# x split tile by tile on GpSimd, and t1 kept centred with its mean beside it, in a two-phase attention and FFN kernel

## The reference

```python
x = einsum('oc,bchw->bohw', inv(I - tpl), x)      # channel mixing by an inverted circulant, "conv"
t = to_tokens(x)                                   # 16 x 1024 tokens x 128
q, k = elu(ln(t) Wq) + 1, elu(ln(t) Wk) + 1;  v = ln(t) Wv         # 8 heads of 16
t = t + causal_linear_attention(q, k, v) @ W_out.T
z = ln(t)
g = mean_over_tokens(relu(z @ gfc1.T + b) @ gfc2.T + b)            # 8 gates for each batch
W1m, W2m = W1 + g . tv_W1, W2 + g . tv_W2                          # weights of their own per batch
t = t + ln(z + relu(z @ W1m.T + b1m) @ W2m.T + b2m) * lng + lnb
```

## Time and profile before

| what | value |
|---|---|
| median of 3 runs | 747.53 us (747.09 to 748.32) |
| the profiled execution | 749.55 us, of which the span of the profile is 747.8 us |
| mean granted TensorE clock | 0.975 |
| busy, of the span | PE 93%, DVE 88%, ACT 87%, POOL 62% |
| first phase at an even pace | 110 to 470 us |
| second phase, first 8 batches | about 500 to 592 us |

### The profile page before, as it was taken

How to read it: one execution, slowest core, us unless ns; L and a number is a source line. 1 busy time by engine, 2 the same in 40 slices (tenths; PEclk the granted TensorE clock), 3 DMA queues, 4 the chain that set the end, 5 groups by cost and what they waited for, 6 DMA issues and landing times. The chain is left out here.

```text
span 747.8 us, 38168 instructions
## 1 busy us (share of the span) xinstructions
PE 692.5 (93%) x12002; PEld 533.8 (71%) x12002; DVE 659.1 (88%) x2409; ACT 649.1 (87%) x1780; POOL 465.2 (62%) x790
## 2 busy tenths in 40 slices
PE   4898899999999999999999999888999998999993
PEld 2576677777777777777777777775777787777772
DVE  5697889999999999999999999768898977998983
ACT  4797989999999999999999999557888876888883
POOL 3686778888888888888888888421333321333333
PEclk9798999999999999999999999899999999999998
DMA  4757676666666666666666666410222211222221
GB/s 149 112 110 134 132 129 129 148 143 131 148 142 132 148 141 132 148 141 134 148 139 135 148 142 123 74 51 1 73 85 83 71 58 31 85 70 84 84 84 70
DMA packets 202485, 82.66 MB, mean 111 GB/s; under 512 B 176093, under 2 KB 189824, under 8 KB 202377
## 3 DMA queue, kind: packets, MB, share of 16 engines
q1 hardware_dynamic: 202440, 82.08, 48.3%
HBM read 22.79 MB, written 17.30 MB: 54 GB/s over the span
## 5 line engine op out<-in xcount | busy, mean ns | idle before, releaser
L892 DVE SCALAR_TENSOR_TENSOR scores_lo<-p_a,scores_hi 128x512 f16<-128x512 f32 x256 | 173.3, 683 | 1.7 <-ACT scores_hi L786 1.3
L786 ACT ACTIVATE scores_hi<-p_a 128x512 f16<-128x512 f32 x256 | 156.2, 611 | 9.3 <-PE p_a L623 9.3
L1010 POOL CAST qk_parts<-qk_f 128x512 f16<-128x512 f32 x128 | 78.0, 610 | 50.2 <-issue 24.9
L1442 POOL TENSOR_TENSOR ffn_rstd_shift<-ffn_rstd_shift,consts 128x4 f32<-128x4 f32 x32 | 36.5, 1142 | 109.1 <-DVE ffn_rstd_shift L1400 109.1
L984 POOL TENSOR_TENSOR stats<-stats,consts 128x2 f32<-128x2 f32 (+1 forms) x128 | 88.2, 689 | 17.9 <-DVE stats L925 13.1
L1224 PE MATMUL psb<-merged_W_of_batch,h_hi 128*128 128x128 f16 x512 | 94.5, 220 | 2.2 <-DVE h_lo L1378 1.5
L1378 DVE TENSOR_TENSOR h_lo<-h_f,h_hi 128x512 f16<-128x512 f32 x128 | 95.6, 786 | 1.1 <-ACT h_hi L1280 1.1
L1269 ACT ACTIVATE h_f<-psb,merged_b_of_batch 128x512 f32<-128x512 f32 x128 | 87.2, 709 | 10.3 <-PE psb L1205 8.6
L1225 PE MATMUL psb<-merged_W_of_batch,h_hi 128*128 128x128 f16 x512 | 94.2, 220 | 0.0
L1226 PE MATMUL psb<-merged_W_of_batch,h_lo 128*128 128x128 f16 x512 | 94.1, 220 | 0.0
L1016 POOL TENSOR_TENSOR qk_parts<-qk_f,qk_parts 128x256 f16<-128x256 f32 x128 | 85.9, 671 | 10.2
(11 more groups left out here) (215 smaller groups left out, 2697.5 us busy)
## 6 DMA issues: line engine op xcount, KB each, us to landing
x_f<-in_x SPq DMA_DIRECT2D x32, 256.0 KB, 3.2
t_rows<-t SPq DMA_DIRECT2D x64, 128.0 KB, 1.8
t_back<-t_rows SPq DMA_DIRECT2D x32, 256.0 KB, 2.6
out<-out_tile SPq DMA_DIRECT2D x32, 256.0 KB, 2.1
tv_share<-in_L_ffn_tv_W SPq DMA_DIRECT2D x32, 128.0 KB, 2.2
qkT_parts<-qk_parts SPq DMA_TRANSPOSE x128, 3.1
zT_hi_lo<-z_parts SPq DMA_TRANSPOSE x128, 2.3
merged_W<-in_L_ffn_W SPq DMA_DIRECT2D x2, 256.0 KB, 4.4
```

The costliest lines, as they stand in the source:

```text
L786: nc.scalar.activation(ah[:, t % 2, cols], p_a[:, cols], ACT.Relu).then_inc(ahi_ready[eo], 1)
L892: nc.vector.scalar_tensor_tensor(al[:, t % 2, cols], p_a[:, cols], 0.0, ah[:, t % 2, cols], ALU.max, ALU.subtract).then_inc(alo_ready[eo], 1)
```

## The change

Four edits.

1. `split_x` leaves ScalarE. GpSimd now makes both parts, one tile at a time and with skew -1, that is for the tile of the next slot: `x_hi` (a cast, 128 x 128) and `x_lo` (a subtraction, 128 x 128) in each slot. GpSimd's loop ends one batch earlier for that, and the last batch is written out.
2. The inverse is centred over its output channels (`centred_inverse` was there already for the projections), W_out has the mean of each row taken off, and one more column holds those means. `out_project` so gives t1 less its mean in columns 0 to 127 and its mean in column 128. `conv` uses the same centred columns.
3. ScalarE's z is then one product of t1 with rstd, with no bias; the stage `shift2` on DVE goes, with its semaphore.
4. In the second phase `add_up` is four operations of 128 x 128, each t1 + mean + normed. The rows of t1 in DRAM are 129 wide.

The lists of ScalarE and VectorE are also put in another order.

```diff
-SCALAR_ORDER = [("normalise", 10), ("split_x", 0), ("relu_qk", 2), ("read_t1", 7), ("gate_relu", 14),
-                ("exp_qk", 1), ("state_hi", 3), ("v_hi", 1), ("tv_hi", 0), ("scores_hi_0", 4), ("copy_out", 6),
-                ("scores_hi_1", 4)]
+SCALAR_ORDER = [("relu_qk", 2), ("normalise", 10), ("read_t1", 7), ("gate_relu", 14), ("v_hi", 1), ("tv_hi", 0),
+                ("state_hi", 3), ("exp_qk", 1), ("scores_hi_0", 4), ("copy_out", 6), ("scores_hi_1", 4)]
...
-        woT = sb(top, "w_outT", [P, C])
+        woT = sb(top, "w_outT", [P, C + 1])
...
-            yt = sb(early, "t1", [P, TILES, C])
+            yt = sb(early, "t1_centred_and_mean", [P, TILES, C + 1])
...
+                    nc.vector.scalar_tensor_tensor(wbig[:, 4 * C:4 * C + 1], pa[:, 1, 0:1], WSI, wbig[:, 3 * C:3 * C + 1],
+                                                   ALU.mult, ALU.subtract)
                     dve.wait_ge(s_wtc, 1)
-                    nc.vector.tensor_scalar(woT[:, :], wsqT[:, 3, :], WSI, None, ALU.mult)
+                    link(nc.vector.tensor_reduce(v[:, 15:16], wsqT[:, 3, :], AX.X, ALU.add))
...
+                    link(nc.vector.tensor_scalar(woT[:, C:C + 1], v[:, 15:16], WSI / C, None, ALU.mult))
+                    nc.vector.tensor_scalar(woT[:, 0:C], wsqT[:, 3, :], WSI, woT[:, C:C + 1], ALU.mult, ALU.subtract)
...
-                        o, cols = p_m1[:, 0:P], slice(j * P, (j + 1) * P)
-                        mm(o, xh[:, hf, cols], wh[:, 0:C], start=True, stop=False)
+                        o, cols = p_m1[:, 0:C + 1], slice(j * P, (j + 1) * P)
+                        mm(o, xh[:, hf, cols], wh[:, 3 * C:4 * C + 1], start=True, stop=False)
...
-                        nc.scalar.activation(xh[:, hf, cols], xf[:, hf, cols], ACT.Copy).then_inc(xh_ready, 1)
...
-                        act.wait_ge(shift_ready, n + 1)
+                        act.wait_ge(rstd, n + 1 + PAIRED)
                         at_least(act, zlo_ready, n - 1)
-                        nc.scalar.activation(z_[:, t % 2, :], yt[:, t, :], ACT.Identity, bias=st2[:, (t + 3) % 4, SHIFT:SHIFT + 1],
-                                             scale=st2[:, (t + 3) % 4, RSTD:RSTD + 1]).then_inc(z_ready, 1)
+                        nc.scalar.activation(z_[:, t % 2, :], yt[:, t, 0:C], ACT.Copy, scale=st2[:, (t + 3) % 4, RSTD:RSTD + 1])\
+                            .then_inc(z_ready, 1)
...
-                    def split_x(b, t):
-                        if t % 2 or isinstance(b, int) and TILES * b + t == 0:
+                    def x_hi(b, t):
...
+                        if j == 0:
+                            pool.wait_ge(x_loaded[hf], loaded)
+                        at_least(pool, wo_done, used)
+                        nc.gpsimd.tensor_copy(xh[:, hf, cols], xf[:, hf, cols]).then_inc(xh_ready, 1)
+                    def x_lo(b, t):
...
+                        pool.wait_ge(xh_ready, n + 1)
                         nc.gpsimd.tensor_tensor(xl[:, hf, cols], xf[:, hf, cols], xh[:, hf, cols], ALU.subtract)\
                             .then_inc(xl_ready, 1)
...
-                        nc.vector.tensor_tensor(rn[:, hf, :, :], rn[:, hf, :, :], t1b[:, hf, :, :], ALU.add)\
-                            .then_inc(v_ready, 1)
+                        for j in range(HALF):
+                            last = nc.vector.scalar_tensor_tensor(rn[:, hf, j, :], t1b[:, hf, j, 0:C], t1b[:, hf, j, C:C + 1],
+                                                                  rn[:, hf, j, :], ALU.add, ALU.add)
+                        last.then_inc(v_ready, 1)
```

More of the change, by code:

```diff
@@ L43 @@
                 ("gate", 13), ("project", 0)]
-SCALAR_ORDER = [("normalise", 10), ("split_x", 0), ("relu_qk", 2), ("read_t1", 7), ("gate_relu", 14),
-                ("exp_qk", 1), ("state_hi", 3), ("v_hi", 1), ("tv_hi", 0), ("scores_hi_0", 4), ("copy_out", 6),
-                ("scores_hi_1", 4)]
[L47 to L50, removed]
+SCALAR_ORDER = [("relu_qk", 2), ("normalise", 10), ("read_t1", 7), ("gate_relu", 14), ("v_hi", 1), ("tv_hi", 0),
+                ("state_hi", 3), ("exp_qk", 1), ("scores_hi_0", 4), ("copy_out", 6), ("scores_hi_1", 4)]
+VECTOR_ORDER = [("make_qk", 2), ("tv_lo", 1), ("divide", 6), ("stats2", 7), ("v_lo", 2), ("stats1", 0),
+                ("mean_var2", 7), ("mean_var1", 0), ("state_lo", 3), ("scores_lo_0", 4), ("denominator", 5),
+                ("scores_lo_1", 4), ("invert", 5)]
+GPSIMD_ORDER = [("rsqrt", 1), ("z_hi", 10), ("x_hi", -1), ("z_lo", 10), ("qk_hi", 2), ("x_lo", -1), ("qk_lo", 2),
                 ("last_rsqrt2", 8)]
@@ L146, in build @@
         delta2h = sb(top, "delta2_f16", [P, GB, FI], F16)
-        wh = sb(top, "w_in_hi", [P, 4 * C], F16)
-        wl = sb(top, "w_in_lo", [P, 4 * C], F16)
-        woT = sb(top, "w_outT", [P, C])
+        wh = sb(top, "w_in_hi", [P, 4 * C + 1], F16)
+        wl = sb(top, "w_in_lo", [P, 4 * C + 1], F16)
+        woT = sb(top, "w_outT", [P, C + 1])
         gfh = sb(top, "gate1_hi", [P, C], F16)
@@ L349, in _ @@
                     act.wait_ge(x_loaded[0], 16)
-                    nc.scalar.activation(xh[:, 0, 0:2 * P], xf[:, 0, 0:2 * P], ACT.Copy).then_inc(xh_ready, 1)
+                    nc.scalar.activation(xh[:, 0, 0:2 * P], xf[:, 0, 0:2 * P], ACT.Copy).then_inc(xh_ready, 2)
                     act.wait_ge(ln_done, 1)
@@ L438, in batch, with run @@
                         behind(TILES * (b - B) + slot)
-            def run(eng, order, stages, behind=None):
+            def run(eng, order, stages, behind=None, upto=B):
                 stages = [(skew, stages[name]) for name, skew in order]
@@ L443, in run @@
                     batch(stages, b)
-                with eng.Fori(2, B) as b:
+                with eng.Fori(2, upto) as b:
                     batch(stages, b)
-                for b in range(B, B + 2):
-                    batch(stages, b, behind)
-            MEAN, VAR, RSTD, SHIFT = 9, 10, 11, 12
+                for b in range(upto, B + 2):
+                    batch(stages, b, behind if b >= B else None)
+            MEAN, VAR, RSTD = 9, 10, 11
             PAIRED = 7
@@ L748, in read_t1 @@
                         act.wait_ge(wo_done, n + 1)
-                        nc.scalar.activation(yt[:, t, :], p_m1[:, 0:P], ACT.Copy, scale=1.0 / WSI).then_inc(t1_ready, 1)
+                        nc.scalar.activation(yt[:, t, :], p_m1[:, 0:C + 1], ACT.Copy, scale=1.0 / WSI).then_inc(t1_ready, 1)
                     def v_hi(b, t):
@@ L823, in merged_w1_hi @@
                             .then_inc(mhi_ready, 1)
-                    run(act, SCALAR_ORDER, {"tv_hi": tv_hi, "split_x": split_x, "read_t1": read_t1, "v_hi": v_hi,
+                    run(act, SCALAR_ORDER, {"tv_hi": tv_hi, "read_t1": read_t1, "v_hi": v_hi,
                         "exp_qk": exp_qk, "relu_qk": relu_qk,
@@ L966, in _ @@
                     run(dve, VECTOR_ORDER, {"tv_lo": tv_lo, "stats1": stats1, "mean_var1": mean_var1, "v_lo": v_lo,
[L967 removed]
+                        "make_qk": make_qk, "state_lo": state_lo,
                         "scores_lo_0": scores_lo(0), "scores_lo_1": scores_lo(1), "denominator": denominator,
@@ L1045, in _ @@
                     run(pool, GPSIMD_ORDER, {"rsqrt": rsqrt, "qk_lo": qk_lo,
-                        "split_x": split_x,
-                        "last_rsqrt2": last_rsqrt2, "qk_hi": qk_hi, "z_hi": z_hi, "z_lo": z_lo})
+                        "x_hi": x_hi, "x_lo": x_lo,
+                        "last_rsqrt2": last_rsqrt2, "qk_hi": qk_hi, "z_hi": z_hi, "z_lo": z_lo}, upto=B - 1)
         with ExitStack() as pb:
```

81 lines of the change are left out of this document (37 added, 44 removed).

## The result

The changed kernel takes **757.29 us** (median, 755.58 to 758.23), the kernel before 747.92 us on the same chip. The ratio is **1.0129** (95% interval 1.0109 to 1.0148). The forecast was 732 us with a range of 719 to 754, so it had the wrong sign and missed by 25 us. The profiled execution took 758.23 us with a span of 756.4 us, which is 8.6 us more than the span before. Medians here are of the fast executions; one of the ten of e4 was slow (880.8 us, granted clock 0.665) and is left out.

What follows compares the result with a forecast made beforehand. It took ScalarE, with DVE and PE 2 to 3% behind, to bound the first phase, and a ring of DVE and GpSimd the second. -21 + 5.6 + 0.5 = -15 us from 747.53 gave 732 us, range 719 to 754.

Steps and rivals of the forecast that it cites:

- PE's need: First phase: PE could do a slot in 3.20 us (3.16 to 3.25), the rest of its 3.48 being waiting.
- 3.20 by starts, 3.33 by durations: First phase: two sums for GpSimd's work per slot after the change; 3.25 us was taken, ends 3.20 and 3.45.
- the half that I counted as won: First phase, DVE: tv_lo's hold-up by GpSimd, 0.10 us on a mean slot, of which half, 0.05 us, was counted as won.
- four engines between 3.19 and 3.25 us to a slot of 3.30: First phase: the engines' needs overlap imperfectly, so a slot takes 3.30 us for 3.48, a gain of 0.18.
- the whole first term: First phase: the shorter slot, over 128 slots, saves 21 us (-7 to -30).
- +0.18 taken: Second phase: four additions for one lengthen each step by 0.18 us, 31 steps, +5.6 us (+5 to +16).
- The bound of +0.52: Second phase: upper bound per step for the four additions, from four full durations of 0.28 us, 1.12 in all.
- Set-up: Ahead of the first projection: four more small DVE operations cost +0.5 us (0 to 1).
- GpSimd becomes the bound: Rival, first phase: GpSimd's work and waits fill a slot of 3.53 us, so the run takes 760 us, slower; chance 0.18.
- the ring: Second phase: DVE's list and GpSimd's power wait on each other, setting the step of 6.54 us; add_up is on it.

Runs made afterwards that it cites:

- e4: The changed kernel with the four additions of the second phase taking a constant 0.0 in place of the mean from SBUF: 751.57 us, ratio 1.0045.
- e9: The whole changed kernel with z transposed by pairs of tiles, four transposes a batch for eight: 735.63 us, ratio 0.9824.
- e1: The kernel before with t1 stored tile by tile, eight stores a batch for four, the same bytes: 780.9 us, ratio 1.043.
- e8: The kernel before with x split ahead on GpSimd, the new list orders and z transposed by pairs; second phase and shift as before: 723.95 us, ratio 0.9659.
- e5: The changed kernel with t1 stored by four tiles, two stores a batch for four: 747.01 us, ratio 0.9971 against the changed kernel.
- e7: The kernel before with z transposed by pairs of tiles, four transposes a batch for eight, of twice the size: 742.07 us, ratio 0.9902.

## Why the prediction was wrong

- **The durations of three engines' work held, PE's seems to have been read too low.** Per slot of 3.47, ScalarE is busy 3.27 (I said 3.19, end 3.29), VectorE 3.25 (3.21, end 3.30), GpSimd 3.15 (3.20 by starts, 3.33 by durations). PE's need was put at 3.20, end 3.25, from two slots; in e9, where nothing but PE is over 98% busy, it is busy 3.29 of a slot of 3.32. The ends of matmuls are modelled, so this is no exact need, but it is above my 3.25. ScalarE's z takes 425 ns on a mean for 514 before (110 to 440 us):

```profile
L791 ACT ACTIVATE z<-t_centred_and_mean,stats 128x128 f32<-128x128 f32 x95 | 40.3, 425 | 0.0
```

- **tv_lo was held up less, not never.** Lines view, 110 to 440 us, before and then after (busy us, mean ns):

```profile
L850 DVE SCALAR_TENSOR_TENSOR tv_lo<-tv_share,tv_hi 128x128 f32 x48 | 24.9, 519 | 0.0
```

```profile
L840 DVE SCALAR_TENSOR_TENSOR tv_lo<-tv_share,tv_hi 128x128 f32 x48 | 19.8, 413 | 0.0
```

  0.28 us is the undisturbed one, so the hold-up fell from 0.24 to 0.13 on a mean, though GpSimd is busier: about the half that I counted as won. The Trainium skill (SBUF — State Buffer, Who interferes with whom) says that a VectorE instruction with two SBUF inputs and a GpSimd instruction that reads SBUF contend for a shared pair of ports, and that whichever issues first keeps the other out. By that rule the place in the list counts and not GpSimd's busy share alone, and the two rows agree with it.
- **The step that failed is the one from four engines between 3.19 and 3.25 us to a slot of 3.30.** It took the five rows of the page for all that can be full. The issuing queue of SyncE needs 27.5 us of a batch of 27.9, or 3.44 us a slot, and it was in the trace before. I wrote of the stores that "they have slots of time, and I count nothing". A store's landing has that time. Its place on the queue has none: e1 priced it at 0.65 us. With the queue full, the whole first term fell away: -21 us became -4 (by the first `add_up`, set-up included), and these 4 lie mostly outside the even part: in the trace 2.3 us in the second batch (29.9 for 32.2). Which edit wins them I did not test. Once the queue has room the slot is 3.33 and 3.32 (e8, e9), close to the 3.30. That is in part luck: the 3.30 stood for engines of 3.20 that overlap imperfectly, and what came is a PE that is busy for 3.29.
- **add_up was mis-sized: +0.18 taken, +0.45 measured**, +13 us for +5.6. The bound of +0.52 held it. I took the start-to-start distance of a two-input operation with a constant scalar (0.19), and for such operations it held: e4's four stand 0.20 us apart and cost +0.20. What I left out is the scalar read from SBUF. I had no row for it in such an operation and did not bound it by itself; it is 0.06 for each of the four, which then stand 1.05 / 4 = 0.26 us apart.
- **Set-up**: the first cast of q and k starts 0.7 us later (20.94 for 20.26) where 0.5 was said.
- **The rival "GpSimd becomes the bound", 760 us, is near the time by chance.** Its mechanism did not come: GpSimd is busy 327 of 360 us, its new operations stand back to back, and it idles for z. The waits on qk_parts that it foretold do show up (11.2 us in the row above), but what they wait for is the transpose's turn on the queue: in e5, with two stores less and the same GpSimd list, they fall to 3.1 us. e9 has the same GpSimd list and a slot of 3.32.
- **What I would have needed**: SyncE's timeline beside those of the other engines, and the product of issues and spacing, 24 a batch. It was one view away.

With both terms as measured in the trace the sum closes, as it must, since they are read from the same two executions: -4 for a first phase held by the queue, +13 for the ring, 749.55 + 9 = 758.6, against 758.23.

## What to carry to other kernels

Count the DMA-issuing queue as one more engine before work is moved off another one: number of issues times the distance of their starts, against the period of the loop. Where two limits coincide, an edit that lifts one of them shows little or nothing, so an edit without effect isn't yet a wrong one; try it with the other limit lifted. And where a vector operation is split or gets an operand of another kind on a ring, multiply its price by the steps of the ring before anything is counted as won elsewhere.

## What the hardware showed that I had not expected

- A DMA transpose holds SyncE's issuing queue for 1.17 us (128 x 256 float16), 1.20 (128 x 512, e7) and 1.23 (q and k, 128 x 1024), so nearly the same for four times the size; a plain DMA for 0.34 to 0.39. Between the end of one issue and the start of the next there are another 0.18 to 0.28 us in the rows above (0.59 once a batch). On this queue one transpose of two tiles of z took 1.20 us in place of twice 1.17.
- A scalar_tensor_tensor of 128 x 128 with two SBUF inputs takes 279 ns with a constant scalar and 340 ns with one read from SBUF.
- Four of them in a row stand 0.20 us apart with the constant and 0.26 with the scalar from SBUF, so it is the operand and not the like successor that sets them apart: the constant form ahead of an operation of another kind stood 0.19 ahead.
